# RGCN with a mixture of experts: four relations as seven half-size products each, and the edge sort in two relations

## The reference

```python
def rgcn(x, edge_index, edge_type, weight, root, bias):
    src, dst = edge_index[0], edge_index[1]
    msgs = x[src]
    out = x @ root + bias
    for r in range(R):
        mask = (edge_type == r).astype(x.dtype)
        sums = segment_sum(msgs * mask[:, None], dst, num_segments=N)
        cnt = segment_sum(mask, dst, num_segments=N)
        out = out + (sums / maximum(cnt, 1.0)[:, None]) @ weight[r]
    return out
# x = layernorm(x); u = rgcn(x); z = [u, x] @ w_gate + b_gate; x += tanh(u) * z + x * (1 - z)
# then: layernorm, top 2 of 8 experts by softmax, SwiGLU experts (1024 -> 256 -> 1024), weighted sum, x +=
```

## Time and profile before

| | |
|---|---|
| median of 3 runs | 1882.14 us (1881.85 to 1883.3) |
| the profiled execution's own time | 1879.97 us |
| its span, first to last instruction | 1877.9 us |
| PE busy | 1760.9 us, 94% |
| DVE, ACT, POOL busy | 962.8, 595.3 and 639.2 us |
| mean granted TensorE clock | 0.973 of full speed |

### The profile page before, as it was taken

How to read it: one execution, slowest core, us unless ns; L and a number is a source line. 1 busy time by engine, 2 the same in 40 slices (tenths; PEclk the granted TensorE clock), 3 DMA queues, 4 the chain that set the end, 5 groups by cost and what they waited for, 6 DMA issues and landing times. The chain is left out here.

```text
span 1877.9 us, 22607 instructions
## 1 busy us (share of the span) xinstructions
PE 1760.9 (94%) x8113; PEld 1448.1 (77%) x8113; DVE 962.8 (51%) x1166; ACT 595.3 (32%) x850; POOL 639.2 (34%) x535
## 2 busy tenths in 40 slices
PE   7999999999999999999999999999889967999993
PEld 6888888888888888888777777777668855787882
DVE  8545555655410110010079999998889976434300
ACT  2211111111111111111156656655532212455451
POOL 1000000000166666610055555555355523545531
PEclk9999999999999999999999999999989977999997
DMA  5222222222532222222188888888754445777645
GB/s 199 90 96 90 79 74 73 84 73 79 171 106 92 93 84 90 84 84 89 62 279 265 302 269 294 265 269 281 239 213 168 157 155 197 191 218 187 160 82 152
DMA packets 122552, 292.80 MB, mean 156 GB/s; under 512 B 16084, under 2 KB 32516, under 8 KB 122384
## 3 DMA queue, kind: packets, MB, share of 16 engines
q1 hardware_dynamic: 80592, 161.17, 24.3%
q0 software_dynamic: 41872, 130.44, 23.7%
HBM read 213.92 MB, written 82.76 MB: 158 GB/s over the span
## 5 line engine op out<-in xcount | busy, mean ns | idle before, releaser
L585 PE MATMUL banks<-whi,xhi 128*128 128x512 f32 x1280 | 502.0, 392 | 0.6 <-DVE xlo L473 0.6
L586 PE MATMUL banks<-wlo,xhi 128*128 128x512 f32 x1280 | 498.9, 390 | 0.0
L587 PE MATMUL banks<-whi,xlo 128*128 128x512 f32 x1280 | 498.9, 390 | 0.0
L732 POOL DMA_INDIRECT gathered<-Y,edge_row x184 | 220.8, 1200 | 317.5 <-PE banks L846 180.7
L309 ACT ACTIVATE y_out<-banks 128x512 f32<-128x512 f32 x160 | 95.5, 598 | 717.8 <-PE banks L587 717.8
L358 DVE TENSOR_TENSOR wlo<-w_stage,whi 128x1024 fp32r<-128x1024 f32 x66 | 80.7, 1224 | 459.6 <-ACT whi L301 458.9
L585 PEld LDWEIGHTS banks<-whi,xhi 128*128 128x128 f32 x1280 | 240.8, 188 | 50.6 <-DVE xlo L473 1.2
L587 PEld LDWEIGHTS banks<-whi,xlo 128*128 128x128 f32 x1280 | 240.7, 188 | 50.3
L586 PEld LDWEIGHTS banks<-wlo,xhi 128*128 128x128 f32 x1280 | 240.8, 188 | 49.0
L751 ACT ACTIVATE ghi<-gathered,edge_w 128x1024 fp32r<-128x1024 f32 x184 | 211.3, 1152 | 170.1 <-DMA gathered<-Y,edge_row 164.6
L789 DVE SCALAR_TENSOR_TENSOR glo<-gathered,edge_w,ghi 128x1024 fp32r<-128x1024 f32 x184 | 232.2, 1281 | 42.8 <-ACT ghi L751 42.3
(11 more groups left out here) (254 smaller groups left out, 2385.5 us busy)
## 6 DMA issues: line engine op xcount, KB each, us to landing
Y<-y_out SPq DMA_DIRECT2D x160, 256.0 KB, 2.0
w_stage<-in_L_gnn_weight SPq DMA_DIRECT2D x62, 512.0 KB, 3.6
raw<-in_L_ffn_w SPq DMA_DIRECT2D x24, 1024.0 KB, 9.4
YX<-y_out SPq DMA_DIRECT2D x40, 256.0 KB, 5.1
w_stage<-in_L_gnn_w_gate SPq DMA_DIRECT2D x12, 512.0 KB, 7.0
X<-x SPq DMA_DIRECT2D x11, 512.0 KB, 3.0
acc<-in_L_gnn_bias POOLq DMA_DIRECT2D x10, 512.0 KB, 10.3
u<-YX SPq DMA_DIRECT2D x10, 512.0 KB, 5.0
```

The costliest lines, as they stand in the source:

```text
L585: pe.matmul(psum[slot][:], xhi[:, k, at], whi[h][:, k], start=(k == 0), stop=False)
L586: pe.matmul(psum[slot][:], xhi[:, k, at], wlo[h][:, k], start=False, stop=False)
L587: ins = pe.matmul(psum[slot][:], xlo[:, k, at], whi[h][:, k], start=False, stop=(k == KC - 1))
L732: nc.gpsimd.indirect_dma_start(out=gath[:, t % GR], out_offset=None, in_=Y, in_offset=bass.IndirectOffsetOnAxis(ap=edge_row[:, t:t + 1], a ...
```

## The change

Relations 0 to 3 are multiplied as before. For relations 4 to 7, x and the weights are cut into 2 by 2 blocks (5 tiles of rows by 4 steps of k, and 4 steps of k by 512 columns), and a relation is seven products of such blocks, by the scheme of Strassen and Winograd: four products take sums of weights, four take sums of x, and results are added up partly in the banks (`more`), partly by VectorE (`sum_tile`).

- The sums of weights: `t_load` and `t_store` on GpSimd bring 32 steps of 512 KB (two DMAs in, two out) through three buffers to `TW` in HBM; VectorE computes them in place (`t_make`), two steps behind each of the first 16 groups of the sort.
- The sort has 12 groups per relation, in relations 1 and 2; TensorE adds each one up inside a product. The second multiplication no longer waits for the first.
- The sums of x: `both` and `less_hi` on VectorE, `sum_hi` on ScalarE, beside relation 3 and the first product. One of them overwrites a quarter of xhi and xlo, which SP stores to `X21` at the start of relation 1 and reads back when 25 of the 28 products are done.
- The new stage has 28 products (n, SN = 28) of five tiles (i). Its weights come in chunks of 256 KB through three places of `raw_chunk` into a ring of two halves, split by `chunk_hi` and `chunk_lo`. `copy` (ScalarE) and `sum_tile` bring the results to SBUF, `store_quarter` (SP) stores them.
- The bias goes into `acc` at products 24 and 26 instead of behind the sort; VectorE waits for it in block 2. Root weights for block 2 are split in the last product. Block 2 has its gathered rows, root weights and `ghi` at other addresses and is otherwise the same.
- Loops over relations on all engines are written out. The loads and stores of the block keep their sizes otherwise.

```diff
 Y = dram("Y", (R * NP, D))
+R0 = R // 2
+HN = NP // 2
+TW = dram("TW", ((R - R0) * D, D))
...
 z2b = Zone(z2.at, LIMIT - z2.at)
-CPQ = 7
-SORT_R = ECOLS // (8 * CPQ)
-assert SORT_R * 8 * CPQ == ECOLS
+CPQ, SORT_R = 7, 2
+SG1 = ECOLS // (SORT_R * CPQ)
...
 inv = z2b.put("inv", [P, BT], F32)
+TS, TQ = 3, HALF // 2
...
+KH, TR = KC // 2, NT // 2
...
+s1sum = quarter(xlo_sum, 1, 0)
+LEFT = ((quarter(xhi, 0, 0), quarter(xlo, 0, 0)), (quarter(xhi, 0, 1), quarter(xlo, 0, 1)),
+        (s2hi, s2lo), (quarter(xhi, 1, 0), quarter(xlo, 1, 0)), (s4hi, s4lo), (s3hi, s3lo),
+        (quarter(xhi, 1, 1), quarter(xlo, 1, 1)))
+CHAIN_A, ALONE, CHAIN_B, CHAIN_C = (0, 1, 2, 3, 4), (5, 6, 7, 0, 1), (2, 3, 4, 5, 6), (7, 0, 1, 2, 3)
+PRODUCT_BANKS = (CHAIN_A, CHAIN_A, ALONE, CHAIN_B, CHAIN_B, CHAIN_C, CHAIN_C)
+FIRST_HALF = R0 * 2 * NT
+def right(n, k):
+    r, p = R0 + n // 7, n % 7
+    w = TW[(r - R0) * D:(r - R0 + 1) * D, :] if p in (2, 3, 5, 6) else weight[r]
+    low, wide = p in (1, 4, 5, 6), p in (3, 4, 5)
+    return w[low * HALF + k * P:low * HALF + (k + 1) * P, wide * HALF:(wide + 1) * HALF]
...
+                    if last and h == 0 and j == NT - 2:
+                        sp.wait_ge(w_lo, R0 * 8)
+                        for c in range(raw_n):
+                            load_raw(c)
+                    if last and h == 1 and j < 8:
+                        load_raw(raw_n + j)
+        def load_raw(c):
+            n, k = c // KH, c % KH
+            if c >= raw_n:
+                sp.wait_ge(q_lo, c - raw_n + 1)
+            if c == 2 * KH:
+                for i in range(TS):
+                    sp.wait_ge(t_moved[i], t_stored[i])
+            sp.dma_start(raw[:, c % raw_n], right(n, k)).then_inc(raw_in[c % raw_n], 16)
...
+        def store_quarter(n, i):
+            s, p = n // 7, n % 7
+            at, done = (R0 + s) * NP + i * P, s * 5 * TR + i + 1
+            if p == 1:
+                sp.wait_ge(copied, (2 * s + 1) * TR + i + 1)
+                sp.dma_start(Y[at:at + P, 0:HALF], half_v[i][:]).then_inc(row_moved[i], 16)
...
         relation(0, first=True)
-        with sp.Fori(1, R - 1) as r:
-            relation(r)
-        relation(R - 1, last=True)
+        sp.wait_ge(lo_done, 2 * NT)
+        for a, part in enumerate((xhi, xlo)):
+            sp.dma_start(X21[a].rearrange("p (k n) -> p k n", n=HN),
+                         quarter(part, 1, 0).bitcast(F32)).then_inc(x21_moved, 16)
+        for r in range(1, R0):
+            relation(r, last=(r == R0 - 1))
+        for n in range(SN):
+            ahead = [c for c in range(KH * (n + 2) - 1, KH * (n + 3) - 1) if KH * 3 - 1 <= c < KH * SN]
+            if n == SN - 3:
+                sp.wait_ge(tile_done, TR * (SN - 3))
+                for a, part in enumerate((xhi, xlo)):
+                    sp.dma_start(quarter(part, 1, 0).bitcast(F32),
+                                 X21[a].rearrange("p (k n) -> p k n", n=HN)).then_inc(x21_moved, 16)
+            for i in range(TR):
+                if i < len(ahead):
+                    load_raw(ahead[i])
+                store_quarter(n, i)
+                if n == SN - 2 and i == 2:
...
                         root_of(j + 4)
-                    if j in after:
+                    if last and h == 1:
+                        if j in (3, 6):
+                            sum_hi((3, 6).index(j))
+                        if j < 8:
+                            chunk_hi(j)
...
+        def chunk_hi(c):
+            n, k = c // KH, c % KH
+            act.wait_ge(raw_in[c % raw_n], 16 * (c // raw_n + 1) + raw_first[c % raw_n])
+            if c == 0:
+                act.wait_ge(y_ready, FIRST_HALF - NT)
+            if n >= 2 and k == 0:
+                act.wait_ge(tile_done, TR * (n - 1))
...
+        for n in range(SN):
+            for i in range(TR):
+                if 1 <= n < SN - 1 and i < KH:
+                    chunk_hi(KH * (n + 1) + i)
+                if n == SN - 1 and i < 4:
+                    root_part(i)
+                if n % 7 < 2:
+                    copy(n, i)
+                if n == 0 and i in (2, 4):
+                    sum_hi(i // 2 + 1)
...
-            equal(oh_klo[:], P, key_lo)
-            dve.wait_ge(hot_ready, (r - 1) * 16 + 2 * part + 1)
-            times(oh_val[:, :, 1], val_dst).then_inc(hot_ready, 1)
-            dve.wait_ge(hot_ready, (r - 1) * 16 + 2 * part + 2)
-            ins = times(oh_val[:, :, 0], val_src)
-            ins.then_inc(cols_ready, 1)
+            equal(oh_klo[:], P, key_lo).then_inc(cols_ready, 1)
+            dve.wait_ge(hot_ready, g + 1)
+            for n, column in ((1, val_dst), (0, val_src)):
+                ins = v.tensor_tensor(oh_val[:, :, n], oh_val[:, :, 0].bitcast(F32),
+                                      column[:, at].unsqueeze(2).to_broadcast([P, CPQ, ET]), ALU.mult)
+            ins.then_inc(vals_ready, 1)
+        def t_make(*steps):
+            sets = [[t_set[:, m % TS, a, b] for a in range(2) for b in range(2)] for m in steps]
+            for m, (b11, b12, b21, b22) in zip(steps, sets):
+                dve.wait_ge(t_moved[m % TS], 64 * (m // TS) + 32)
+                v.tensor_tensor(b22, b22, b12, ALU.subtract).then_inc(t_made, 1)
+                v.tensor_tensor(b12, b12, b11, ALU.subtract).then_inc(t_made, 1)
+            at = 4 * steps[0]
+            for m, (b11, b12, b21, b22) in zip(steps, sets):
+                dve.wait_ge(t_made, at + 2 * (m - steps[0]) + 1)
+                v.tensor_tensor(b11, b22, b11, ALU.add).then_inc(t_made, 1)
+            for m, (b11, b12, b21, b22) in zip(steps, sets):
+                dve.wait_ge(t_made, at + 2 * len(steps) + m - steps[0] + 1)
+                v.tensor_tensor(b21, b21, b11, ALU.subtract).then_inc(t_made, 1)
...
             for h in range(2):
-                for q in range(4):
+                for part in range(SG1 // 2):
                     if sorts:
-                        columns(r, 4 * h + q, first and h * 4 + q == 0)
-                    if not (start and h == 0):
-                        split_lo(*((r, 1) if h == 0 else (r + 1, 0)), q)
+                        g = (r - 1) * SG1 + h * SG1 // 2 + part
+                        columns(r, h * SG1 // 2 + part, g == 0)
+                        if 2 * g < T_STEPS:
+                            t_make(2 * g, 2 * g + 1)
+                    if part in SPLIT_PARTS and not (start and h == 0):
+                        split_lo(*((r, 1) if h == 0 else (r + 1, 0)), SPLIT_PARTS.index(part))
...
+        def chunk_lo(c):
+            n, k = c // KH, c % KH
+            dve.wait_ge(q_hi, c + 1)
+            v.tensor_tensor(ring_lo[n % 2][:, k], raw[:, c % raw_n], ring_hi[n % 2][:, k].bitcast(F32),
+                            ALU.subtract).then_inc(q_lo, 1)
...
+        def less_hi(m, hi, low, total):
+            dve.wait_ge(s_hi, m + 1)
+            both(low, total, hi, ALU.subtract).then_inc(s_ready, 1)
+        (a11h, a11l), (a12h, a12l), (a21h, a21l), (a22h, a22l) = LEFT[0], LEFT[1], LEFT[3], LEFT[6]
+        for r in range(1 + SORT_R, R0):
+            for q in range(4):
+                split_lo(r, 1, q)
+            if r < R0 - 1:
+                for q in range(4):
+                    split_lo(r + 1, 0, q)
+        for i in range(TS):
+            dve.wait_ge(t_moved[i], t_stored[i])
+        dve.wait_ge(inv_out, 16)
+        step(both(s4sum, a21h, a21l, ALU.add))
+        step(both(s4sum, s4sum, a22h, ALU.add))
+        step(both(s4sum, s4sum, a22l, ALU.add))
+        chunk_lo(0)
+        step(both(s2sum, s4sum, a11h, ALU.subtract))
+        both(s2sum, s2sum, a11l, ALU.subtract).then_inc(s_raw, 1)
+        chunk_lo(1)
+        chunk_lo(2)
+        less_hi(0, s2hi, s2lo, s2sum)
+        chunk_lo(3)
+        dve.wait_ge(s_ready, 1)
+        step(both(s4sum, a12h, s2hi, ALU.subtract))
+        step(both(s4sum, s4sum, s2lo, ALU.subtract))
+        both(s4sum, s4sum, a12l, ALU.add).then_inc(s_raw, 1)
+        chunk_lo(4)
+        chunk_lo(5)
+        less_hi(1, s4hi, s4lo, s4sum)
...
+        def sum_tile(n, i):
...
+            dve.wait_ge(tile_done, TR * n + i + 1)
+            if p == 2:
+                dve.wait_ge(copied, 2 * s * TR + i + 1)
+                ins = v.tensor_tensor(half_u[i][:], bank[:], half_u[i][:], ALU.add)
+            if p == 3:
...
+        for n in range(SN):
+            for i in range(TR):
+                if 1 <= n < SN - 1 and i < KH:
+                    chunk_lo(KH * (n + 1) + i)
+                if n == SN - 1 and i < 4:
+                    root_low(i)
+                if n % 7 >= 2:
+                    sum_tile(n, i)
...
+        def t_load(m):
+            if m >= TS:
+                pool.wait_ge(t_moved[m % TS], 64 * (m // TS))
+            s, k, part = m // 8, m // 2 % KH, m % 2
+            for a in range(2):
+                rows_of = weight[R0 + s][a * HALF + k * P:a * HALF + (k + 1) * P, :]
+                pool.dma_start(t_set[:, m % TS, a], rows_of.rearrange("p (b n) -> p b n", b=2)
...
```

(121 more changed lines are left out.)

205 lines of the change are left out of this document (155 added, 50 removed).

## The result

The kernel after took 1871.03 us in the median of 6 runs (1867.42 to 1876.08), the kernel before 1882.72 in 6 runs (1881.69 to 1886.55). The medians are 11.7 us apart; the ratio of the runs is 0.9927, with a 95% interval of 0.9911 to 0.9944, which stands for 13.7 us of 1882. So it is faster clear of the noise, though by less than 1%, where 48.2 us were forecast, and 1871 lies above the range of 1828 to 1869. The profiled execution has a span of 1869.8 us where 1829.7 was worked out: **40.1 us** have to be found.

A forecast was written before the change was run, and what follows sets the result against it. TensorE, busy 94% of the span, was taken to bound the kernel, paid in matmuls up to 935 us. -54.4 (matmuls) + 5.7 (sort waits) + 0.5 (block's end) = -48.2 us, giving 1834 us; range 1828 to 1869.

The forecast's parts named there:

- What it removes: Relations 4 to 7: 1680 matmuls instead of 1920, 240 fewer at 0.2267 us each, -54.4 us.
- VectorE's own turn: Sort: VectorE's work per group, 11.16 us with a split and 10.0 without, beside TensorE's 10.62; alone costs under 1 us.
- The ring: Weight chunks of the half-size products: ready with 3.6 us to spare, no wait; falling short was a rival, +28 us, chance 0.07.
- product 2: Sums of x needed after relation 3: ready after 25 us, product starts at 27.2, so hidden with 2 us to spare.
- The quarter of x: Stored at relation 1, 2.6 MB read back later: nothing; 2 us if read back late, 8 us once if store cover fails.
- issue beside a busy VectorE: Rival, sort: GpSimd's DMA issues take 0.24 us more each, chain 12.01 us, waits 19 us, 1847 us; chance 0.08.
- the landing of the stores in the chain of the sort: Sort's weight-sum transfers: landing taken as 3.2 us, bounds 2.5 and 4.6; chain 11.05 us, +5.7 us of waits.
- landings near 4 us: Rival, sort: landings of 3.6 to 4.4 us; at 4.0 chain 12.65, waits 28.7, 1857 us (1845 to 1869); chance 0.20.
- slower than before: Outcome in the chances, whole kernel: changed kernel slower than the kernel before, chance 0.07.
- the last rival: Sort: landings of 4.6 us, 47 us of waits plus 1.3 us of clock each, 1895 us; left out of the range.
- The end of the block: Change to the next block: last sum 0.1 us longer and more semaphores for SP, +0.5 us.
- GpSimd is in nobody's way: Behind the sort: gathers end near 716 us, bias loads go out from product 24 (about 830), so no cost.

The follow-up runs named there:

- e7: Kernel after with four `t_set` buffers, last two root loads first, and one bias load copied by ScalarE instead of ten loads; 1829.45 us, ratio 0.9708.
- e1: Kernel after without the stores of the weight sums and loads past the first three steps, using relations' own weights (Y wrong); 1843.09 us, ratio 0.9774.
- e2: Kernel after with a fourth `t_set` buffer for the weight sums, all transfers kept; 1844.97 us, ratio 0.9777.
- e4: e3 with the quarter of x read back on GpSimd's queue behind the bias, instead of on SP's; 1862.72 us, ratio 0.987.
- e5: e3 with one bias tile loaded at product 24 and copied to the other nine by ScalarE, in place of ten loads; 1858.7 us, ratio 0.9864.
- e3: Kernel after with the last two root-weight loads ahead of the last product's stores on SP, VectorE's remainders paired to match; 1864.97 us, ratio 0.9874.
- e8: e7 with the last two root loads going to `w_early` after four stores, not behind two splits; 1830.98 us, ratio 0.9718.
- e6: e2 with e3's order: four `t_set` buffers and the last two root loads first; 1836.65 us, ratio 0.9745.

## Why the prediction was wrong, by its own steps

**Right.** *What it removes*: in e7, where TensorE waits only 0.4 us in block 1, the last product matmul starts at 879.68; 934.45 less the 54.4 is 880.05. *VectorE's own turn* hides (e1, e2). *The ring* and *product 2*: no such line in the waits of TensorE, and 390.00 of 390 us busy. *The quarter of x*: nothing (another queue for it changes nothing in e4, and e5 and e7, which still read it back on SP, end the block with a wait of 3.3 us, where the kernel before has 3.24). `t_make` took 2.95 us by the sum, and 2.84 by the timeline, 153.55 to 156.39. Of the rivals, *issue beside a busy VectorE* didn't come: a pair of loads took 1.44 us at 174.97, with VectorE busy throughout, and 1.41 at 191.46, with VectorE idle.

**The step that failed most: the landing of the stores in the chain of the sort.** The prediction said "I take 3.2, near to the idle row, because only one other pair is ahead of it", counted from the end of the issue. One of the late turns, in the timeline of GpSimd:

```profile
181.50 2.79 POOL L843 DMA_DIRECT2D TW<-t_set  x4 [3.51 <-DVE t_set L562]
188.71 1.44 POOL L835 DMA_DIRECT2D t_set<-in_L_gnn_weight  x2 [4.42 <-DMA TW<-t_set]
191.46 1.41 POOL L835 DMA_DIRECT2D t_set<-in_L_gnn_weight  x2 [1.30 <-DMA TW<-t_set]
196.64 2.80 POOL L843 DMA_DIRECT2D TW<-t_set  x4 [3.77 <-DVE t_set L562]
```

and of VectorE:

```profile
194.24 0.43 DVE L554 TENSOR_TENSOR t_set<-t_set 128x256 f32<-128x256 f32 x1 [4.35 <-DMA t_set<-in_L_gnn_weight]
```

Half of 2.79 us issues the first pair of stores, until 182.90; they have landed at 188.71, 5.8 us later. The two loads are issued by 190.15, and VectorE has them at 194.24, 4.1 us later; then the six operations, and the next stores at 196.64. The turn is 1.4 + 5.8 + 1.4 + 4.1 + 2.4 = 15.1 us, where the forecast had 1.2 + 3.2 + 1.2 + 3.2 + 2.25 = 11.05. Only the first turn is longer. The one ahead of this, and every third from there, is short, because its stores had landed 2.4 us after the issue of their pair:

```profile
171.16 2.79 POOL L843 DMA_DIRECT2D TW<-t_set  x4 [4.76 <-DVE t_set L562]
174.97 1.44 POOL L835 DMA_DIRECT2D t_set<-in_L_gnn_weight  x2 [1.01 <-DMA TW<-t_set]
```

From the second group's stores (156.77) to the last (335.95) there are 14 turns, five of 10.3 to 11.1 us and nine of 13.3 to 15.1; why it is every third isn't settled. Their mean is 2.84 + 4.39 + 3.17 + 2.40 = 12.80 us: issues, landing of the stores, landing of the loads, operations. So the loads landed in the 3.2 us that were forecast; the stores took 1.2 longer than that, the issues 0.4 (0.70 instead of 0.6 per DMA) and the operations 0.15. 1.75 us more per turn is what turned 5.7 us of waits into 28.8. Over the whole stretch the medians, from issue to landing of a single 256 KB, are these:

```profile
t_set<-in_L_gnn_weight POOLq DMA_DIRECT2D x63, 256.0 KB, 3.6
TW<-t_set POOLq DMA_DIRECT2D x60, 256.0 KB, 5.5
Y<-y_out SPq DMA_DIRECT2D x28, 256.0 KB, 5.6
```

The result stores of SP, no part of the change, went from 2.0 us to 5.6 in this stretch. I had the load right (190 + 74 = 264 GB/s worked out, 237 measured) and wrote that it is near to that of the next block, but then took the landing of an idle queue, since "here the chain itself limits what is in flight". The row for full engines was in hand: the 5.8 us of the gathers, which is my upper bound of 4.6 from the end of issue; the stores' mean of 4.39 is close to it. The rival *landings near 4 us* had the sort right: its chain is 12.65 us, where the mean turn is 12.80, and it gave 28.7 us of waits, where 28.8 were lost. It is right in the sum and not in the parts, since it has loads and stores alike (and its 1857 lacks what went at the block's end).

**The clock fell too, and cost nothing of its own.** I priced it only in what the chances call "slower than before" and the range "the last rival": landings of 4.6 us, waits of 3.2 us in each group, 47 us in all, and 1.3 us of clock on top of each wait, for 1895. The 1.3 came from the block's end of the kernel before, where behind 3.24 us of idle time the granted clock was 0.51 from 938.5 to 941 and six starts took 2.69 us, where six at 0.2267 take 1.36. It came with 12 waits, the longest 4.5 us, and the granted clock at 0.50 in three places (202.0 to 208.8, 243.0 to 246.4 and 280.6 to 284.0 us). The longest wait and the group behind it, in TensorE's timeline:

```profile
204.51 2.49 PE L898 MATMUL banks<-oh_val,oh_lo 128*128 128x368 f32 x7 [4.53 <-DVE oh_val L545]
```

The seven matmuls took 2.49 us instead of 1.33. But all that VectorE waited for TensorE in this stretch is one wait in the first turns:

```profile
DVE oh_val L536 <- PE banks L901: 2.7, 1, 2.7
```

Behind it the chain alone sets when the next one-hots are ready, and a slower TensorE only waits less for them. e4 shows it: its waits for the one-hots are 2.7 us shorter than in the kernel after (18.5 to 21.2), it has more at the lower clock (0.96 to 0.97 in the stretch), its mean turn is 12.78 us, and its last product matmul starts at 908.65, to 908.87. So those 1.3 us of clock per wait are not to be added. In e1 and e2, where the waits are gone, the clock is 1.00 throughout; which length of wait brings it down isn't shown, and the length alone doesn't decide: behind the wait of 2.67 us at 277.07 the clock was low, behind that of 2.76 at 315.79 it was not.

**"The end of the block", +0.5, measured +11.9.** I gave one sentence to it and looked at no queue. Two causes, the first taken away by itself, the second on top of it: the order on SP, in which a load waits for a store, that for a sum and that for the remainder of the load before (6.8 us, 15.1 to 8.3, e3); and "the bias loads now go out from product 24 on, so GpSimd is in nobody's way" (5.0 us, 8.3 to 3.3, e5). GpSimd's queue was in nobody's way, the 2.6 MB behind product 26 were: they lay on the DMA engines when the last chunks of the ring were wanted. The landing of these chunks was 9.3 us in the median between 870 and 920 us of the kernel after; over all 64 chunks of `TW` it was 2.8.

**What stays open.** The next block took 416.3 us before and 421.6 after, 419.2 to 423.8 in e1 to e8 (e6 the longest), and 421.2 in e7 (from 883.35 to the last matmul at 1304.5), where the block's end is as short as before. Of those 4.9 us in e7, 3.2 are longer waits for `glo` (22.5 us in 30, before 19.3 in 26) and some 1.6 a stretch of 52 us with a granted clock of 0.97 where before it was 1.00. Why the same instructions wait longer there isn't settled; no run was made for it, the kernel before has one profile, and the eight experiments differ among themselves by 4.6 us. So e7's span of 1829.2 beside the forecast 1829.7 is no proof of the sum: the 5.7 us of waits in the sort did not come, and 6 were lost behind the block's end (4.9 in the next block, 1.2 behind it), where the prediction had nothing. That the two agree is luck.

## What to carry to other kernels

Where a buffer is stored and then filled again, its turn is two landings and two issues long (with the operations between 12.80 us here in the mean), and the landing to use is that of the traffic the change itself makes, taken from a row of a stretch as full as that, and for loads and stores separately. A further buffer was worth 26 us here in the medians (1871.0 to 1845.0, which need not be of one chip) and 28 by the ratios (0.9927 to 0.9777), with the same bytes moved. Where such a chain sets the pace, the clock of an engine that waits for it was not a further cost here (last product matmul at 908.65 in e4, with more at the lower clock, and at 908.87 in the kernel after). And in a program with one queue per engine, cost the end of a block by writing down what the queues hold in its last 20 us: each load behind a store behind a sum is a round trip, and transfers that are "in nobody's way" share the DMA engines with those that are: the last chunks landed in 3.4 us with one bias load (e5) and in 8.0 with ten (e3).

## What the runs showed of the hardware

- Landings under load: 256 KB took 2.0 us on SP's queue at 74 to 100 GB/s (before and e1) and 5.6 at 237 GB/s, with the DMA engines at 0.72 of their time. Loads into SBUF on GpSimd's queue were shorter (3.6) than stores out of it (5.5); in e2, at 257 GB/s, they were 4.1 and 5.7.
- The granted clock fell to 0.50 (202.0 to 208.8 us, for one) in a stretch that was mostly busy: 185.72 of 204 us, with 12 waits of up to 4.5 us. How long it stayed there at the block's end didn't follow the idle time of TensorE. Behind 15.1 us of idle time it was 0.50 until 4.6 us after the first start (912.0 to 929.0), in e2 behind 15.1 until 4.4 after it (882.6 to 899.6), in e5 behind 3.3 until 5.6 (909.95 to 916.7), in e7 behind 3.3 until 3.0 (882.95 to 886.35). In e8, behind 3.3 too, it was 1.00 at the first start (883.26) and 0.50 only from 883.85 to 887.25.
- A direct DMA of GpSimd with 256 rows of 1 KB took 0.70 to 0.72 us to issue, with VectorE busy (174.97) or idle (191.46); those of the bias, with other shapes, took 0.52. VectorE was busy for 185.21 us with 253 operations beside 128 such issues (e2) and for 185.04 with 252 beside 6 (e1): it was not held up. GpSimd instructions that read SBUF were not compared beside a busy VectorE.
